# A decoder block on one Trainium2 core: attention work lists rewritten on every engine, and eight transposes moved inside a product

## What is computed

```python
x = x + attn(_layernorm(x))        # 16 heads of 64, causal softmax, then y @ w_o
x = x + xattn(_layernorm(x), ctx)  # 64 context rows for each sequence, masked softmax
x = x + ffn(_layernorm(x))
# ffn: h = silu(w1 x) * (w2 x); h = gelu(h1 h); h = gelu(h2 h); out = w3 h
```

## Time and profile before

| | before |
|---|---|
| median of 3 runs | 1447.77 us |
| profiled execution, its time | 1446.44 us |
| profiled execution, its span | 1444.7 us |
| PE busy | 1424.8 us (99%) |
| DVE / ACT / POOL busy | 84% / 70% / 42% |
| mean granted clock of TensorE | 0.997 |

### The profile page before, as it was taken

How to read it: one execution, slowest core, us unless ns; L and a number is a source line. 1 busy time by engine, 2 the same in 40 slices (tenths; PEclk the granted TensorE clock), 3 DMA queues, 4 the chain that set the end, 5 groups by cost and what they waited for, 6 DMA issues and landing times.

```text
span 1444.7 us, 29203 instructions
## 1 busy us (share of the span) xinstructions
PE 1424.8 (99%) x10408; PEld 1230.6 (85%) x10408; DVE 1210.4 (84%) x3004; ACT 1010.2 (70%) x2382; POOL 603.2 (42%) x883
## 2 busy tenths in 40 slices
PE   8999999999999999999998999999999999999998
PEld 7888888888888888888887778888888888888887
DVE  7998998989989999898899767888776748888886
ACT  7888888888888888888887855564456445555644
POOL 4766776776767677676744121111111100000000
PEclk9999999999999999999999999999999999999999
DMA  4000101001001010010022544543442583041311
GB/s 162 2 1 2 60 1 38 24 2 59 2 16 45 2 60 1 2 60 2 16 74 74 186 154 146 197 159 126 146 136 99 209 316 118 31 147 60 118 54 36
DMA packets 78277, 113.54 MB, mean 79 GB/s; under 512 B 4768, under 2 KB 54304, under 8 KB 77216
## 3 DMA queue, kind: packets, MB, share of 16 engines
q1 hardware_dynamic: 78112, 111.32, 22.6%
HBM read 71.45 MB, written 42.99 MB: 79 GB/s over the span
## 4 chain that ended last, share of the span: by engine, by line
PE 90%; DVE 5%; ACT 3%; issue 1%; POOL 1%; DMA 0%; DVEq 0%
PE bank L1606 14%; PE bank L957 10%; PE bank L929 8%; PE bank L877 8%; PE bank L1433 8%; PE bank L878 7%; PE bank L879 7%; PE bank L1435 7%; PE bank L941 5%; PE bank L1624 4%; PE bank L1560 2%; PE bank L1551 2%; PE bank L1553 2%; PE bank L1549 2%; ACT P L1011 1%; PE bank L1443 1%
## 5 line engine op out<-in xcount | busy, mean ns | idle before, releaser
L1011 ACT ACTIVATE P<-P,stats 128x256 f32<-128x256 f32 (+3 forms) x512 | 289.8, 574 | 105.5 <-DVE stats L1113 104.1
L1143 POOL TENSOR_SCALAR P<-P,stats 128x512 f32<-128x512 f32 (+3 forms) x512 | 269.0, 543 | 111.4 <-DVE stats L1121 109.3
L1113 DVE CUSTOM_DVE_ANT_0 P<-bank,cmask 128x256 f32<-128x256 f32 (+3 forms) x512 | 217.0, 486 | 1.5 <-PE bank L929 0.4
L1027 DVE TENSOR_TENSOR PT<-bank,PT 128x512 fp32r<-128x512 f32 (+1 forms) x384 | 206.6, 592 | 5.6 <-ACT PT L980 4.6
L1606 PE MATMUL bank<-op,ws 128*128 128x512 f32 x896 | 205.9, 390 | 0.0
L1433 PE MATMUL bank<-Hb,hw 128*128 128x512 f32 x512 | 202.3, 395 | 0.8 <-DVE Hb L1809 0.8
L1606 PEld LDWEIGHTS bank<-op,ws 128*128 128x128 f32 x896 | 167.4, 188 | 34.0
L957 PEld LDWEIGHTS bank<-PT,V 128*128 128x128 f32 x1024 | 162.3, 190 | 19.1 <-DVE PT L1027 3.9
L980 ACT ACTIVATE PT<-bank 128x512 fp32r<-128x512 f32 (+1 forms) x384 | 173.0, 528 | 5.8 <-PE bank L941 5.6
L1435 PE MATMUL bank<-Hb,hw 128*128 128x512 f32 x448 | 175.5, 392 | 0.0
L957 PE MATMUL bank<-PT,V 128*128 128x512 f32 (+3 forms) x1024 | 171.7, 320 | 2.9 <-DVE PT L1027 2.9
(11 more groups left out here) (247 smaller groups left out, 3209.0 us busy)
## 6 DMA issues: line engine op xcount, KB each, us to landing
h_scratch<-go SPq DMA_DIRECT2D x64, 256.0 KB, 2.1
src<-h_scratch SPq DMA_DIRECT2D x16, 1024.0 KB, 7.4
xs<-x_scratch SPq DMA_DIRECT2D x15, 512.0 KB, 4.1
ws<-ws_scratch SPq DMA_DIRECT2D x7, 1024.0 KB, 7.8
x_scratch<-x SPq DMA_DIRECT2D x8, 512.0 KB, 3.0
x_scratch<-xs SPq DMA_DIRECT2D x8, 512.0 KB, 3.4
xg<-x_scratch SPq DMA_DIRECT2D x8, 512.0 KB, 4.0
out<-xg SPq DMA_DIRECT2D x16, 256.0 KB, 2.1
```

The costliest lines, as they stand in the source:

```text
L1011: e.activation(p, p, ACT.Exp, bias=st_[:, k:k + 1], scale=-1.0, accum_out=st_[:, 8 + k:9 + k]).then_inc(s_exp, 1)
L1027: return e.tensor_tensor(dst, a, b.bitcast(f32), ALU.subtract)
L1113: e.tensor_tensor_reduce(P_tile(P, i, a), banks["S", P, S_ITEM[i]][a][:, slice(*S_COLS[i])], cmask[:, 512 - n:512], -1.0, 3.0e38, ALU.add, ...
L1143: e.tensor_scalar(p, p, stats[P % 4][:, k:k + 1], 1.0, ALU.mult, ALU.mult).then_inc(s_norm, 1)
```

## The change

The lists of `ATTENTION` are written anew for PE, ACT, DVE and POOL, with the same steps in another order; SP's stays. 184 of PE's 809 places, 724 of ACT's 1286, 904 of DVE's 1487 and 493 of POOL's 809 hold another step. In the steady part PE's list is in both kernels `k v q AV AV O S S S T T T` for most pairs; steps change places by one or two. Pairs that share a bank for S and T go from 60 to 61 (pair 62 comes in). The places where PE's list changes most, shortened:

```diff
-idle.0 rows.0.0 rows.0.1 idle.1 k.0 q.0 v.0 S.0.3 S.0.2 S.0.1 k.1 q.1 v.1 v.2 v.3 S.1.3 S.1.2 T.0.0
+idle.0 idle.1 rows.0.0 rows.0.1 k.0 q.0 v.0 S.0.3 S.0.2 S.0.1 k.1 q.1 v.1 v.2 S.1.3 v.3 S.1.2 S.1.1
...
-xc xs.0 AV.62.0 AV.62.1 O.61 xpt.0 T.63.0 T.63.1 T.63.2 xo.0.0 xo.0.1 O.62
-AV.63.0 xv.2 AV.63.1 xv.3 xt.0.1.0 xt.0.1.1 O.63 ft.2 g.0.0 u.0.0 g.0.1 O.64
+xc xs.0 AV.62.0 AV.62.1 T.63.0 T.63.2 T.63.1 xv.2 xpt.0 xv.3 xo.0.0 xo.0.1 AV.63.0
+AV.63.1 O.61 O.62 xt.0.1.0 xt.0.1.1 O.63 ft.2 O.64 g.0.0 u.0.0 g.0.1
...
-g.0.7 ft.3 u.0.7
+g.0.7 u.0.7 ft.3
```

On ACT `wh.1` comes before the two `rows_high`, on DVE `wl.0 wl.1` before the two `rows_low`. On ACT `xe.0` moves behind `yo.62`, `ph.63.0.0`, `big.6` and two more `ph.63`. On DVE `os.61` moves from ahead of `xpl.0` to behind `xtl.0.1.1`, and `flag.3` from behind `hl.0.1` to behind `hm.0.7`; `hm.0.0` comes after `fl.9` to `fl.11`, four `os` and two `xvl`. The rest of the diff, whole:

```diff
@@ -1418,12 +1417,24 @@
             w.wait_ge(s_found, FLAGS.index(k) + 1)
             e.transpose(out[0:1, 0:128], flags[:, 2 * k:2 * k + 1], ident[:, :]).then_inc(s_ft, 1)
 
-        def hidden(out, src, m, ready, new=None, scores_of=0):
+        def transpose_rows(b, which, j):
+            out, = claim(w, ("xt", b, which, j))
+            if (b, which, j) == (0, 1, 0):
+                keep_warm(e, out, 22)
+            w.wait_ge(s_ln2, ln_at(b, which) + 4)
+            for t in range(NT):
+                i = e.transpose(out[:, t * 128:t * 128 + 128], xns[:, t, j * 128:j * 128 + 128], ident[:, :])
+            i.then_inc(s_x2T, 1)
+
+        def hidden(out, src, m, ready, new=None, scores_of=0, rows_of=0):
             for c in range(8):
                 if c == 4 and scores_of:
                     scores_by_rows(scores_of)
                 if c == 5 and new == 0:
                     transpose_flag(0)
+                if c == 5 and rows_of:
+                    for j in range(2):
+                        transpose_rows(rows_of, 1, j)
                 hidden_step(out, src, m, ready, c)
             return hidden_end(out, src, m, new)
 
@@ -1466,14 +1477,8 @@
                             c == 0, c == 1)
                 i.then_inc(s_xv, 1)
             elif kind == "xt":
-                b, which, j = a
-                out, = claim(w, item)
-                if a == [0, 1, 0]:
-                    keep_warm(e, out, 22)
-                w.wait_ge(s_ln2, ln_at(b, which) + 4)
-                for t in range(NT):
-                    i = e.transpose(out[:, t * 128:t * 128 + 128], xns[:, t, j * 128:j * 128 + 128], ident[:, :])
-                i.then_inc(s_x2T, 1)
+                if a[:2] != [1, 1]:
+                    transpose_rows(*a)
             elif kind == "xf":
                 js = slice(a[0] * 128, a[0] * 128 + 128)
                 out, = claim(w, item)
@@ -1581,7 +1586,8 @@
                     hidden_end(out, src, 1).then_inc(s_hid, 1)
                 else:
                     hidden(out, src, m, ready, 0 if (b, m) == (0, 3) else None,
-                           b + 1 if m == (3 if b == 0 else 1) and b + 1 < B else 0).then_inc(s_hid, 1)
+                           b + 1 if m == (3 if b == 0 else 1) and b + 1 < B else 0,
+                           1 if (b, m) == (0, 7) else 0).then_inc(s_hid, 1)
             elif kind == "prod":
                 p, i, m = a
                 out, = claim(w, item)
```

More of the change, by code:

```diff
@@ L37 @@
+        T.3.1 v.7 k.5 q.5 rows.1.0 rows.1.1 AV.3.0 AV.3.1 O.2 S.5.3 S.5.2 S.5.1 T.4.2 T.4.1 T.4.0 v.8 k.6 q.6
+        AV.4.0 AV.4.1 O.3 S.6.3 S.6.2 S.6.1 T.5.2 T.5.0 T.5.1 v.9 k.7 q.7 AV.5.0 AV.5.1 O.4 S.7.3 S.7.2 T.6.0
+        S.7.1 T.6.2 T.6.1 k.8 q.8 v.10 AV.6.0 AV.6.1 O.5 S.8.3 S.8.2 S.8.1 T.7.2 T.7.0 T.7.1 k.9 q.9 v.11
+        AV.7.0 AV.7.1 O.6 S.9.3 S.9.2 T.8.0 S.9.1 T.8.2 T.8.1 k.10 v.12 q.10 AV.8.0 AV.8.1 O.7 S.10.3 S.10.2
         S.10.1 T.9.2 T.9.0 T.9.1 k.11 v.13 q.11 AV.9.0 AV.9.1 O.8 S.11.3 S.11.2 S.11.1 T.10.2 T.10.0 T.10.1
-        k.12 v.14 q.12 AV.10.0 AV.10.1 O.9 S.12.3 S.12.2 S.12.1 T.11.2 T.11.0 T.11.1 v.15 k.13 q.13 AV.11.0
@@ L67 @@
+        q.45 AV.43.0 AV.43.1 O.42 S.45.3 S.45.2 S.45.1 T.44.2 T.44.0 T.44.1 k.46 v.48 q.46 AV.44.0 AV.44.1
+        O.43 S.46.3 S.46.2 S.46.1 T.45.2 T.45.0 T.45.1 k.47 v.49 q.47 AV.45.0 AV.45.1 O.44 S.47.3 S.47.2
+        S.47.1 T.46.2 T.46.0 T.46.1 k.48 v.50 q.48 AV.46.0 AV.46.1 O.45 S.48.3 S.48.2 S.48.1 T.47.2 T.47.0
         T.47.1 k.49 v.51 q.49 AV.47.0 AV.47.1 O.46 S.49.3 S.49.2 S.49.1 T.48.2 T.48.0 T.48.1 k.50 v.52 q.50
@@ new lines @@
+        ph.34.2.1 ph.34.1.0 kh.36 e.35.2.1 vc.38 e.35.2.0 qh.36 e.35.1.0 e.35.1.1 yo.34.0 e.35.0.0 yo.34.1
+        e.35.0.1 e.36.3.0 e.36.3.1 ph.35.0.0 ph.35.0.1 ph.35.1.1 ph.35.2.0 ph.35.2.1 ph.35.1.0 kh.37 e.36.2.0
+        vc.39 e.36.2.1 qh.37 e.36.1.0 e.36.1.1 yo.35.0 e.36.0.1 yo.35.1 e.36.0.0 e.37.3.0 e.37.3.1 ph.36.0.1
+        ph.36.0.0 ph.36.1.0 ph.36.2.0 ph.36.2.1 ph.36.1.1 kh.38 e.37.2.1 vc.40 e.37.2.0 qh.38 e.37.1.1
+        e.37.1.0 yo.36.0 e.37.0.1 yo.36.1 e.37.0.0 e.38.3.1 e.38.3.0 ph.37.0.1 ph.37.0.0 ph.37.1.0 ph.37.2.0
@@ new lines @@
+        ph.37.2.1 ph.37.1.1 kh.39 e.38.2.1 vc.41 e.38.2.0 qh.39 e.38.1.1 e.38.1.0 yo.37.0 e.38.0.0 yo.37.1
+        e.38.0.1 e.39.3.0 e.39.3.1 ph.38.0.1 ph.38.0.0 ph.38.1.1 ph.38.2.0 ph.38.2.1 ph.38.1.0 kh.40 e.39.2.0
+        vc.42 e.39.2.1 qh.40 e.39.1.0 e.39.1.1 yo.38.0 e.39.0.1 yo.38.1 e.39.0.0 e.40.3.1 e.40.3.0 ph.39.0.0
+        ph.39.0.1 ph.39.1.0 ph.39.2.0 ph.39.2.1 ph.39.1.1 kh.41 e.40.2.0 vc.43 e.40.2.1 qh.41 e.40.1.1
+        e.40.1.0 yo.39.0 e.40.0.0 yo.39.1 e.40.0.1 e.41.3.0 e.41.3.1 ph.40.0.0 ph.40.0.1 ph.40.1.1 ph.40.2.0
@@ new lines @@
+        ph.58.0.1 e.59.2.1 ph.58.1.0 ph.58.1.1 kh.60 e.59.0.1 e.59.1.1 qh.60 yo.58.0 yo.58.1 e.59.0.0 vc.62
+        e.60.3.1 e.60.3.0 ph.59.0.1 ph.59.2.1 ph.59.2.0 ph.59.0.0 ph.59.1.1 ph.59.1.0 e.60.2.0 e.60.2.1
+        e.60.0.1 kh.61 qh.61 vc.63 yo.59.0 yo.59.1 e.60.1.1 e.60.1.0 e.60.0.0 e.61.0.0 ph.60.2.1 e.61.0.1
+        e.61.2.0 ph.60.2.0 e.61.3.1 kh.62 ph.60.0.0 ph.60.0.1 ph.60.1.0 e.61.3.0 e.61.2.1 ph.60.1.1 xth.0.0.0
+        xth.0.0.1 qh.62 yo.60.0 e.61.1.1 yo.60.1 e.61.1.0 ph.61.2.0 ph.61.2.1 fh.0 fh.1 ph.61.0.1 e.62.3.0
@@ new lines @@
+        ph.61.1.0 ph.61.0.0 ph.61.1.1 kh.63 fh.2 e.62.0.0 qh.63 e.62.2.1 fh.3 e.62.1.1 e.62.0.1 e.62.3.1
+        e.62.2.0 bqh xkh.0 xkh.1 e.62.1.0 fh.4 fh.5 fh.6 e.63.2.1 yo.61.0 yo.61.1 e.63.2.0 e.63.3.1 e.63.3.0
+        xfh.0 xfh.1 big.5 e.63.0.0 ph.62.0.0 ph.62.1.1 xvh.0 e.63.1.0 ph.62.0.1 ph.62.2.1 ph.62.2.0 ph.62.1.0
+        xcc e.63.0.1 e.63.1.1 fh.7 yo.62.0 yo.62.1 ph.63.0.0 xvh.1 big.6 ph.63.1.1 ph.63.0.1 xe.0 ph.63.2.0
+        ph.63.2.1 xph.0 ph.63.1.0 fh.8 yo.63.0 yo.63.1 big.7 big.8 fh.9 xth.0.1.0 xth.0.1.1 fh.10 fh.11 xvh.2
```

639 lines of the change are left out of this document (306 added, 333 removed).

## The result

| | before | after |
|---|---|---|
| median | 1447.99 us (9 runs) | 1451.52 us (9 runs, 1449.57 to 1452.91) |
| ratio to before, 95% interval | | 1.0029 (1.0019 to 1.0040) |
| profiled execution: time, span | 1446.44, 1444.7 us | 1452.91, 1451.1 us |
| mean granted clock of TensorE | 0.997 | 0.993 |

The kernel became 0.29% slower; the forecast was 0.35% faster. One of the nine runs before took 2289.17 us and does not enter the ratio, which is taken from the other runs and is not the quotient of the two medians. In the code after, the lines of the attention have a number smaller by one (L941 is L940); of those behind it L1475 is L1426, L1512 is L1517, L1809 is L1815, L1641 is L1647, L1657 is L1663, and L2152 (the loads `ld`) is L2158.

The account below looks back on a forecast made before the run. PE, busy 99% of the span, was taken as the bound, so only its stands or slow running could be won. Terms -3.9 + 0.3 + 0 - 2.2 + 0.7 = -5.1 us from 1447.77 gave 1442.7 us, range 1438.5 to 1447.5.

Parts of the forecast that it names:

- Part 1: Transposes of xt.1.1 moved inside h.0.7: 3.9 us won from wait, slow matmuls and slow transposes; ends 1.5 to 4.1 won.
- the give-back through `hl.1.7`: At h.1.0, waiting for the last subtraction hl.1.7, the gain could be cut by 0 to 1 us; taken as 0.
- Part 2: Start, with idle.1 ahead of the rows transposes: 0.3 us lost; ends 1.0 won and 2.5 lost.
- Part 3: Steady attention, 11.65 us per pair: 0 change; ends 2 won and 3 lost.
- The rival of a cover lost in every pair: Steady attention: an operand 0.15 us late in each pair costs 8.4 us, giving 1451.1 us; chance 0.08.
- Part 4: End of attention, AV.62 to the norm: 2.2 us won; ends 1 lost and 4.5 won.
- could start near 787: End of attention: walked with old durations, xt.0.1 starts near 787 instead of 791.2; half the gain taken, 2.2 us.
- the 1.4 us that the prediction names: End of attention: extra win if the norm, left at 2.84 us, no longer ran beside POOL's split of Y.
- Part 5: First gated layer, with flag.3 and ft.3 later: 0.7 us lost; ends 0.5 won and 3 lost.
- Uncovered gaps: Waits at the start and at ft.3 drop PE to 1.2 GHz, part 4 winning only 1.4: 1445.6 us; chance 0.24.
- It doesn't do what it says: Moved staging holds DVE or POOL, delaying the xt.1.1 norm; part 1's gain falls to 1.5 us; no separate chance.
- the slower rival: Steady attention loses its cover, 0.15 us in each pair: 1451.1 us; chance 0.08.

Follow-up runs that it names:

- e14_start_new: The kernel before with the xt.1.1 transposes moved inside h.0.7 and only the order of the start new; ratio to the kernel before 1.0023.
- e3_layer_old: The changed kernel with the first gated layer and its staging in the old order; 1444.15 us, ratio to the kernel before 0.9989.
- e9_piece13: The changed kernel with only staging piece 13 (fl.13, fh.13, big.13) moved earlier on VectorE and ScalarE; 1445.21 us, ratio to the kernel before 0.9989.
- e5_end_new: The kernel before with the xt.1.1 transposes moved and only the end of attention in the new order; ratio to the kernel before 1.0000.
- e13_warm_av: The kernel before with the xt.1.1 transposes moved and ten extra transposes ahead of AV.62; ratio to the kernel before 0.9981.
- e19_fl_clear: e3_layer_old with fl.6, fl.7 and big.6 moved back and n.63.0.1 ahead of yl.61 on GpSimd; ratio to the kernel before 0.9987.
- e10_piece13_flag: e9_piece13 with flag.3 also ahead of hm.0.3 on VectorE and ft.3 ahead of u.0.7 on TensorE; ratio to the kernel before 0.9984.

## Why the prediction failed

**Part 1, right.** Forecast 3.9 us, measured 3.9 alone (0.9973). The wait at 845 is gone, the clock stays up, and the give-back through `hl.1.7` is 0, as taken.

**Part 2, near in size, but not a part by itself.** The forecast was 0.3 us lost. The start by itself, ahead of the old pairs, costs 7 us (`e14_start_new`); with the new pairs behind it both together cost 0.0006 of the time, 0.9 us, and 0.7 up to `xs.0` in the trace. That the sum came near is in part luck. `k.0` starts at 11.92 in the changed kernel and between 11.85 and 13.09 in the other traces with the new start; 12.65 was forecast. In the changed kernel the 1.66 us ahead of `k.0` left the clock at 1.00; in two of fifteen traces with this start it fell. The price for that fall, 1.6 us for twelve or more matmuls, looks too low by the rows: 0.43 against 0.23 us makes 2.4 for twelve. A second stand that I did not name, 1.7 us ahead of `T.0` at 30 us, has the clock at 0.64 from 31 to 35 us in the changed kernel and at 1.00 in `e3_layer_old` and `e9_piece13`. That fall is not the new order's alone: with the old start it was 0.57 there in `e5_end_new` and `e13_warm_av`, and 1.00 in the kernel before.

**Part 3, near enough.** Forecast 0; with the start it is 0.0006 of the time, inside the interval. Between `k.10` and `k.57`, ahead of each of which both lists have the same steps, pass 550.1 to 551.5 us in the traces with the new pairs and 552.2 to 552.4 in the four with old start and old pairs: the steady pairs themselves won 1 to 2 us. The rival of a cover lost in every pair did not come: most steps stay at 11.65.

**Part 4, the wrong sign.** `AV.62` did find its operands: in the changed kernel it waits 0.16 us and runs 2.76, where it waited 1.6 us and then ran 4.33. The failed step is "could start near 787": it started at 793.78. I gave the new order only what it removed, walked the rest with the old durations, and halved the result for safety. The old durations did not hold: the scalings beside `fl.6` and `fl.7` take 1.3 us each, not 0.64, and the time that `AV.62` no longer waits is spent ahead of `T.63` and `xpt.0`, with the fall of the clock moved there. I had used the shared interface for the norm alone, not for the scalings that the new order puts beside two full-tile subtractions. Forecast -2.2, measured +0.0010 (1.4 us) on top of the pairs, just at what is told apart, and 1.9 in the trace from `xs.0` to `xt.0.1`.

What I left at 2.84 us, the norm, did fall apart from GpSimd's split of Y in the changed kernel and took half, the 1.4 us that the prediction names:

```profile
790.36 1.38 DVE L1875 TENSOR_SCALAR xns<-xs,sm 128x256 f32<-128x256 f32 x4
791.71 0.62 POOL L1164 TENSOR_SCALAR Y<-Yf 128x512 fp32r<-128x512 f32 x1 [1.58 <-PE bank L878]
```

It won nothing there: the norm is done at 791.7, and TensorE comes to `xt.0.1` only at 793.78, without a wait.

**Part 5, the step that decides.** Forecast +0.7, measured +5.8 us. The two causes I named came: `ft.3` waits 1.6 us ("about 2 us behind PE"), and the list of VectorE is late. What I did not walk is the staging. The prediction counts `fl`, `os` and `xvl` as time on VectorE ahead of `hm.0.0`, and not what a late `fl` sets off: `fl.13`, `big.13`, the buffer, `ld.16`, and with it ScalarE at `fh.16` and all of SyncE's list. Of later stretches it says that their loads "hang on PE's own progress"; of this one it says nothing about loads, and here one load hung on a VectorE instruction moved behind a norm. The 5.97 us of the stand are one part of the 6.5; the half clock behind it adds 2.3 more by the end of `xo.1` (10.4 - 8.1), and some 1.8 are saved, of which 1.3 are the old list's waits there for `hl` (0.77) and xns (0.56).

**The rivals.** "Uncovered gaps" had the right kind (stands long enough for the clock to fall, at two places) and the wrong places. "It doesn't do what it says" names moved staging as the cause, but for the norm of `xt.1.1`, which was not held. No rival had a moved stage step that delays a DMA. The time, 1451.5 us, is nearly that of the slower rival, 1451.1, but by luck: its mechanism, 0.15 us lost in every pair, did not come. The time lies outside the range, and neither of the two signs of being wrong that the prediction gives (a long wait for `hl.1.7`, pairs over 11.8) would have shown it.

## What to carry to other kernels

When an order moves a step that frees a buffer, follow the buffer: which load waits for it, which queue issues that load, and what stands behind both the load's issue and its first use. A load that is late by eleven us holds two engines here, and moving one user away gained next to nothing of 6 us. And lists fitted to one another are not parts: take from such a change the piece that stands on its own (here the move, 3.9 us), and look at what the rest costs without it.

## What the runs showed of the hardware

- A GpSimd scaling of 128x256 that took 0.6 us (1.93 for three) took 1.3 (3.92 for three) beside VectorE subtractions whose two inputs are in SBUF, while these kept their 1.21 us.
- It goes the other way too. A norm of VectorE (four instructions of 128x256) took 1.38 us where GpSimd started behind it (the changed kernel) and 2.83 where a scaling and a subtraction of GpSimd started with it (`e19_fl_clear`), while that scaling kept its 0.63 us.
- What a stand does to TensorE's clock is not settled by its length alone. It stayed at 1.00 behind 1.66 us ahead of `k.0` in the changed kernel, and was 0.50 from 13 to 16 us in `e10_piece13_flag` behind 1.67 us at the same place. Behind 2.03 us at 772 to 774 in the changed kernel 24 transposes still ran at full clock (0.96 us); it fell with the second stand, of 1.33. With the old start, stands of some 1.0, 0.8 and 0.65 us between 25 and 30 us were followed by 0.57 from 31 to 35 us in `e5_end_new` and `e13_warm_av` and by 1.00 in the kernel before. What else enters, no run here shows.
